# A four-layer graph network on one core: the setup moved in among the first units, and half groups shifted by one unit

## What is computed

```python
x = _layernorm(x + _L0_gnn_ref(x, adj, ...))   # attention, 4 heads
x = _layernorm(x + _L1_gnn_ref(x, adj, ...))   # 3 rounds of h = GRU(A^T (h W_l), h)
x = _layernorm(x + _L2_gnn_ref(x, ..., adj, ...))  # one product per relation 1..4
x = _layernorm(x + _L3_gnn_ref(x, adj, ...))   # attention, 1 head
```

## Time and profile before

| | us |
|---|---|
| median of 3 runs | 2815.49 |
| lowest and highest | 2813.47, 2816.87 |
| profiled execution, its own time | 2813.75 |
| its span | 2811.9 |

### The profile page before, as it was taken

The page is one execution under the profiler, slowest core; times in us unless marked ns, Lnnn a source line. Parts: engine busy times, 40 slices in busy tenths (PEclk is TensorE's granted clock), DMA queues, the critical chain, the costliest instruction groups (busy, mean ns, idle before and its releaser), DMA issues.

```text
span 2811.9 us, 48614 instructions
## 1 busy us (share of the span) xinstructions
PE 2686.6 (96%) x15577; PEld 2315.8 (82%) x15577; DVE 2126.9 (76%) x5138; ACT 1663.4 (59%) x4164; POOL 1257.9 (45%) x1351
## 2 busy tenths in 40 slices
PE   3799999999999999999999999999999999999984
PEld 2678888888888888888888888888888888888873
DVE  6466787777788777878778777877777788777754
ACT  0455666666566666666566666656666666666542
POOL 0134544454445445444544544444444444444442
PEclk8699999999999999999999999999999999999995
DMA  7000000000000000000000000000000000000000
GB/s 202 19 20 18 18 24 22 27 24 26 22 21 24 22 28 24 26 22 18 27 22 27 24 26 18 22 24 26 27 24 24 20 22 22 28 28 18 13 10 16
DMA packets 97276, 75.29 MB, mean 27 GB/s; under 512 B 6624, under 2 KB 92768, under 8 KB 96992
## 3 DMA queue, kind: packets, MB, share of 16 engines
q1 hardware_dynamic: 77296, 54.28, 6.7%
q10 hardware_dynamic: 19696, 17.44, 1.9%
HBM read 54.93 MB, written 16.78 MB: 25 GB/s over the span
## 4 chain that ended last, share of the span: by engine, by line
PE 75%; DVE 11%; issue 4%; ACT 2%; POOL 2%; POOLq 0%; DVEq 0%; ACTq 0%
PE psum L757 45%; PE psum L618 9%; PE psum L674 5%; PE psum L654 3%; PE psum L792 3%; PE psum L745 3%; PE psum L744 2%; PE psum L663 2%; PE psum L633 2%; DVE ht_h L1085 2%; DVE y_t L1031 2%; DVE stats L1008 2%; DVE y_t L1132 1%; ACT x L932 1%; DVE moments L1012 1%
## 5 line engine op out<-in xcount | busy, mean ns | idle before, releaser
L1166 POOL TENSOR_SCALAR rstd<-moments 128x2 f32<-128x2 f32 x256 | 78.8, 308 | 999.5 <-DVE moments L1012 999.1
L757 PE MATMUL psum<-ht_h,whh_h 128*128 128x512 f32 x1152 | 481.3, 418 | 0.0
L757 PE MATMUL psum<-ag_h,wc_h 128*128 128x512 f32 x1152 | 478.2, 415 | 0.0
L757 PE MATMUL psum<-ht_h,whh_l 128*128 128x512 f32 x1152 | 456.0, 396 | 0.0
L757 PE MATMUL psum<-ag_l,wc_h 128*128 128x512 f32 x1152 | 455.6, 395 | 0.0
L757 PE MATMUL psum<-ht_l,whh_h 128*128 128x512 f32 x1152 | 455.5, 395 | 0.0
L757 PE MATMUL psum<-ag_h,wc_l 128*128 128x512 f32 x1152 | 454.1, 394 | 0.0
L1221 POOL TENSOR_TENSOR ht<-ht,g_n 128x512 f32<-128x512 f32 x192 | 265.2, 1381 | 151.2 <-ACT g_n L920 148.7
L757 PEld LDWEIGHTS psum<-ht_h,whh_l 128*128 128x128 f32 x1152 | 216.6, 188 | 52.8
L757 PEld LDWEIGHTS psum<-ag_h,wc_l 128*128 128x128 f32 x1152 | 216.3, 188 | 53.0
L757 PEld LDWEIGHTS psum<-ht_l,whh_h 128*128 128x128 f32 x1152 | 217.7, 189 | 38.6
(11 more groups left out here) (150 smaller groups left out, 7044.8 us busy)
## 6 DMA issues: line engine op xcount, KB each, us to landing
adj_i<-in_adj_dram SPq DMA_DIRECT2D x128, 128.0 KB, 2.1
x_in<-in_x_dram SPq DMA_DIRECT2D x64, 256.0 KB, 2.7
out_dram<-out_t ACTq DMA_DIRECT2D x64, 256.0 KB, 2.1
adj_g<-in_adj_dram SPq DMA_DIRECT2D x32, 256.0 KB, 3.8
hh_raw<-in_L_gnn_w_hh_dram SPq DMA_DIRECT2D x1, 768.0 KB, 7.5
ih_raw<-in_L_gnn_w_ih_dram SPq DMA_DIRECT2D x1, 768.0 KB, 11.6
wl_raw<-in_L_gnn_weight_dram SPq DMA_DIRECT2D x1, 768.0 KB, 12.4
wrs<-in_L_gnn_weight_dram SPq DMA_DIRECT2D x1, 768.0 KB, 11.2
```

Source lines behind the costliest of these rows:

```text
L757: last = mm(dst, s, m, start=(first and k == 0), stop=(last_part and k == len(flat) - 1))
```

## The change

1. **No setup block.** Its steps are steps of the same ordered list: `prep_first` (the first attention's weights), `prep_ih`, `prep_wl`, `prep_w3`, `prep_hh` (turnings), `prep_mul` (products), `prep_bias`, `prep_last` (weights of layers 3 and 4), and loads `load_*`. The turnings and products come in pieces of one bank and go through the four banks of the gates (`PREP`), which the GRU doesn't use before the last of them (`gru_hn(0,0,0)` waits for all). A stage copy and a copy of the augmented weights fall away; of the copies out of PSUM half go to ACT.
2. **The scan** of `adj` is 32 parts of 4 graphs with three buffers instead of 8 of 16 with four; each load waits on SP until the part three places back is reduced. The flag is made by `flag` and read by `learn` on four engines, ahead of the first `rel_rest`.
3. **Half groups move by one unit**: half group k holds units 2k-1 and 2k. There are 33; the first holds unit 0 alone and the last unit 63 alone, and their GRU instructions are 256 columns wide.
4. **Three tables**: a new `HALF`, and `FIRST` and `LAST`, which give the first units' and the last units' steps an order of their own.
5. Buffers of the main part are laid where the setup's were, in another order.

```diff
-         "adjg": 1, "nodes": 1, "agg": 1, "adjf": 1, "out": 1, "yr": 1, "yf": 1, "x1": 3}
+         "adjg": 1, "nodes": 1, "agg": 1, "prep": 4, "scan": 3, "adjf": 1, "out": 1, "yr": 1, "yf": 1, "x1": 3}
...
 HALF = """
...
+gru_hn(0,0,1)  gru_split(-1,1)  att_wh(post,-2,0,0)  att_wh(post,-2,0,1)  rel_h1(-2,1)  att_pv(pre,1,0)  gru_turn(-1,1,0)
+        gru_turn(-1,1,1)  gru_n(0,0,0)  att_xt(pre,1,1)  att_exp(pre,1,0)  att_res(pre,1,0)
+gru_rzh(0,0,1)  att_scores(post,-2,0,0)  att_wh(pre,1,1,0)
...
+FIRST = """
+prep_first()  load_first()  pre_load(0)  load_ih()  att_xt(pre,0)  pre_load(1)  att_wh(pre,0,0)  att_wh(pre,0,1)
+        att_scores(pre,0,0)  load_hh()  att_scores(pre,0,1)  att_xt(pre,1)  prep_ih(0)  att_prob(pre,0)  prep_ih(1)
...
-    return [(name,) + kind + (2 * k + a[1],) + a[2:]]
+    u = 2 * k - 1 + a[1]
+    return [(name,) + kind + (u,) + a[2:]] if 0 <= u < 2 * halves - 2 else []
...
-    HALVES = B // 4
+    HALVES, UNITS = B // 4 + 1, B // 2
...
+            def prep_mul(l, j):
+                i = take(pe, "prep", "prep_mul", l, j)
+                prepped(pe, "prep_wl", l)
+                prepped(pe, "prep_ih", j)
+                for n, c in enumerate((j,) if j < C else range(C)):
+                    cols = slice(0, 2 * D) if j < C else slice(2 * D, G3)
+                    dst = PREP[:, i, :] if j < C else PREP[:, i, n * D:(n + 1) * D]
+                    for e in range(C):
+                        last = mm(dst, wlT[:, l, e, c * P:(c + 1) * P], ihT[:, e, cols], start=(e == 0), stop=(e == C - 1))
+                last.then_inc(s_prep_ps, 1)
...
+            def scan(n):
+                i, rounds = ring("scan", "scan", n)
+                dve.wait_ge(s_part[i], 16 * (rounds + 1))
+                nc.vector.tensor_reduce(tops[:, n:n + 1], parts[i][:], AX_XY, ALU.max).then_inc(s_scan, 1)
...
             def gru_hn(k, l, c):
                 if l == 0:
+                    if k == 0:
+                        pe.wait_ge(s_prep_lo, len(PIECES))
                     pe.wait_ge(s_ht0_l, 2 * k + 2)
...
-                accumulate(HN_PS, gate_terms(rows_of(2, c), whh_h, whh_l, ht_h[k % 2], ht_l[k % 2]), True, True).then_inc(s_ph, 1)
+                accumulate(HN_PS[:, nodes_of(k)], gate_terms(rows_of(2, c), whh_h, whh_l, ht_h[k % 2], ht_l[k % 2], nodes_of(k)), True, True).then_inc(s_ph, 1)
```

778 lines of the change are left out of this document (489 added, 289 removed).

## The result

| | before | after |
|---|---|---|
| median, us (4 runs each on one chip) | 2814.93 | 2712.87 (2711.84 to 2714.37) |
| ratio of times, 95% interval | | 0.9637 (0.9621 to 0.9654) |
| profiled execution: span, us | 2811.9 | 2711.9 |
| PE busy in the span | 96% | 98% |
| start of the first aggregation, us | 115.38 | 50.66 |

The forecast was 2744.6 (2714 to 2782). The sign was right; the size, 102 us instead of 71, is just outside the range. The period is the mean distance of every third aggregation between 400 and 2500 us.

A forecast was written before the change was run, and what follows sets the result against it. PE, busy 96% of the span, was taken as the bound: 57 + 2612.3 + 16 + 2.7 + 7 + 46 = 2741 us of span. Adding 1.85 and 1.7 gave a median of 2744.6 us, range 2714 to 2782.

The forecast's parts named there:

- T1: Head: start of half group 0's first aggregation, forecast at 57 us, ends 50 and 74; it was 115.4 before.
- rest of the work: PE's work behind T1: 2623 less 11.8 us already done, plus 1.0 for narrow products, 2612.3 us.
- idle behind T1, head: PE's idle time in the head after the first aggregation starts: 16 us, ends 8 and 28; 11 before.
- flag: Making the adjacency flag and its reading by four engines before the first rel_rest: 2.7 us once, ends 1 and 6.
- middle: PE's idle time over the whole middle: 7 us, ends 0 and 20; 10 before.
- end: last turns and behind: Idle at the end: 9 us in the last three turns, 37 behind the last gate product; together 46, ends 37 and 61.
- That is the price of work when nothing stands still: 32 periods x 81.97 = 2623 us.: Whole kernel: PE's busy time per two-unit period, 81.97 us, taken as the price of dense work, 2623 us in all.
- It is the distance from `rel_h1` to `rel_y1`: Middle: PE's 28 waits for h_l, 9.3 us, laid to this distance; 0.5 us more should all but remove them.
- Rival 1: The head stays at the low clock, 1.2 GHz: T1 = 74, 2762 us; chance 0.15.
- rival 4: It all fits: T1 = 50, 8 in the head, no middle wait, 37 at the end, 2712 us; chance 0.06.
- rival 2: Narrow turns bound by their chain, or DVE by the scan: head 28, end 57, 2767 us; chance 0.15.
- Rival 3: A new wait each period between att_xt and att_wh, 3.5 us, makes it slower, about 2835 us; chance 0.04.

The follow-up runs named there:

- e5: The kernel before with rel_h1 of a half group's first unit one gate group earlier, ahead of g_hn in DVE's list: 2801.28 us, ratio 0.9950.
- e3: The changed kernel with rel_h1 of a half group's first unit one gate group later, nearer to rel_y1: 2715.96 us, ratio 0.9646.
- e4: The changed kernel with each of the 32 scan parts reduced over one of its four graphs, loads whole: 2709.74 us, ratio 0.9625.
- e13: The changed kernel itself, run again without any edit: 2712.44 us, ratio 0.9631.
- e7: The changed kernel with its own head order only up to the first aggregation, the period's order from there: 2726.99 us, ratio 0.9685.
- e15: The changed kernel with products nobody reads in five of PE's gaps behind the last gate product: 2708.16 us, ratio 0.9627.
- e1: The kernel before with rel_y1 and rel_rest behind the aggregation's second half, the next unit's scores one gate group later: 2962.24 us, ratio 1.0522.
- e2: The kernel before with only rel_y1 and rel_rest moved behind the aggregation's second half, scores right behind them: 2949.52 us, ratio 1.0484.
- e10: The changed kernel with 18 unused fp32 products on the identity ahead of unit 0's first transposes: 2711.42 us, ratio 0.9623.
- e14: The changed kernel with start waits and loads rearranged, and the last unit's rel_h1, rel_y1 and norm ahead of the two units before it: 2715.31 us, ratio 0.9642.

## Why the prediction was too small

Its sum, term by term, with what the profile of the changed kernel has (us):

| term | forecast | found |
|---|---|---|
| T1 | 57 | 50.7 |
| rest of the work | 2612.3 | 2597 |
| idle behind T1, head | 16 | 8.5 |
| flag | 2.7 | 2.5 |
| middle | 7 | 0 |
| end: last turns and behind | 9 + 37 | 19.5 + 33.6 |
| span | 2741 | 2711.9 |

**The step that failed** is the first: "That is the price of work when nothing stands still: 32 periods x 81.97 = 2623 us." PE's busy time is the union of modelled durations, 0.39 us for a product whose successor starts after 0.233, so it covers short stands; the changed kernel's is 82.00 in 82 us although its period is 81.49. 32 x 81.49 = 2608 is the price, 15 us less than I took, and with the 7 us that I left for the middle this is 22 of the 29 missed. e5 shows the cause on the kernel before: 0.51 us a period for a reported 0.33. The prediction had the right prices in hand: it added up the head and the end by distances of starts, and by the same prices a period is 216 x 0.233 + 188 x 0.11 + 72 x 0.12 + 8 x 0.22 = 81.4 us (wide products, turns and other narrow pieces, products of 256 to 264 columns, the last attention's values). The step "It is the distance from `rel_h1` to `rel_y1`" was wrong too, though the wait went as forecast: e3 has a shorter distance and no wait. It was the two steps ahead of `h_l` on DVE.

**T1** came out close to DVE's 49 (49.0 to 50.9 in seven profiles with this start), so the 8 us added for hand-overs weren't needed. That DVE was the bound isn't shown: it was busy for 27.5 of 32.6 us from 18 us on ("over 75%" was right), but so was PE for 30.2, and in e4 DVE had less to do and the last 9.8 us stayed the same. **The clock.** Rival 1, 1.2 GHz throughout, is refuted, though the clock wasn't full throughout either. Products of 264 columns were 0.22 us apart from 12.6 us to 15, turns 0.11 apart from 17.8 to 22, then both at the low rate until 26:

```profile
17.79 1.47 PE L682 MATMUL psum<-ident,ih_raw 128*128 128x128 f32 x12
...
25.80 0.42 PE L724 MATMUL psum<-w_h,xt_h 128*128 128x264 f32 x1
26.02 0.34 PE L724 MATMUL psum<-w_l,xt_h 128*128 128x264 f32 x1
26.20 0.28 PE L724 MATMUL psum<-w_h,xt_l 128*128 128x264 f32 x1
```

The Trainium skill (TensorE: Matmul & The Clock Gate, Part 4: PE-mode transpose) says that a transpose doesn't count as busy PE in the same way. For these fp32 turns e13 speaks against it: 36 turns and no product stand between 17.2 and 23.8 us, and all come at the full rate. The changed kernel's own profile doesn't decide it: the rate fell behind 24 of them, and rose 1.0 us after the first product that followed twelve more. What the low stretch cost is 1.7 us of T1; the rival's price of 17 us for a low clock throughout was not tested.

**The head** has 8.5 instead of 16, which is rival 4's value and not rival 2's (an estimated 3 of it are low clock: 0.50 from 67.2 to 73.8 us with PE busy for 6.1): DVE had slack (e4), and the own order keeps away the waits that e7 shows (14 us). Rival 4 as a whole gave 2712, 1 us from the result, and that is luck: its 37 us for the end are 16 below what was found, and the 15 us of the period's price cancel them. **The flag** held. **The end** is right in its sum within 7 us and wrong inside: the last turns have twice what I gave them, and the chain behind is shorter. My sum had no place for the low rate: some 4 us of the chain behind (e15), and more in the last turns, where the granted clock is 0.50 from 2623.8 to 2630.4 us and from 2647.7 to 2657.7 with PE busy for 14.0 of these 16.6 us. An estimated 7 us of the 19.5 are that, if such work takes twice its time there. **Rival 3**, a wait at `att_xt` to `att_wh`, didn't come at its place. But e1 and e2 show the mechanism at another: one step misplaced in DVE's or ACT's list costs 3 to 5 us a period, the low clock behind the new wait included (2.6 of it in e2), as much as I had priced it. I had argued against it with ACT's mean idle time, which says nothing of what stands ahead of one step.

## What to carry to other kernels

Price dense work by the distance of starts, not by the busy time: where a matmul's modelled duration is longer than the distance to its successor, idle time up to the difference is in no row, once per wait. Before moving a step on the bound engine, list for each engine what it will stand behind there; a move by one group that looks free on PE cost 135 to 147 us here through DVE's and ACT's lists, and through the low clock that came with the new waits. At the two ends of a kernel, where PE waits on chains, the low rate behind a gap is a second price of each wait. Work that nobody reads held the rate up in the profiles (e15), but the gain in the measured time isn't clear of its interval.

## What the hardware did that I had not expected

- The full rate of PE outlasted 1.9 us of standing and was gone behind 3.1 us more with four turns between (e10), and behind 4.7 us (e14). The Trainium skill (TensorE: Matmul & The Clock Gate, Why this matters for your kernels) advises against long gaps between bursts; the runs agree.
- The granted clock of a short window can say 1.00 where the products start at half rate: in the changed kernel, 8.6 to 16 us, products of 264 columns lie 0.22 apart, 0.12 later on. From 16 us on the column follows the rate in that profile: 1.00 from 16.0 to 22.6, and 0.50 from 22.8 to 26.0.

```profile
8.60:16.00 7.40, 4.82 (x21) 4.38 (x22) 3.37 (x6) 1.48 (x4) 0.04 (x1) 1.00 1.14 321
```

- Two executions of one kernel can differ in one short stretch of low clock, here 1.7 us at the first aggregation (the changed kernel and e13).
- A DVE step of 0.69 us took 1.65 while POOL's addition of 1.60 us ran beside it (e1).
